# First transfers reordered, identity products ahead of the first product, and one rounding and two diagonal adds moved to VectorE

## The chip, the core and the metric

The kernel runs on one core of a Trainium2 chip. The metric is the time of one execution on the device in microseconds (us). The core's engines are TensorE (PE in the profile; its weight loads are PEld), VectorE (DVE), ScalarE (ACT), GpSimd (POOL) and SyncE (SP). Each has its own instruction stream, and they wait for each other by semaphores. Loads are issued by SP's queue, the first one and two small ones by ScalarE's.

## What is computed

Four residual layers act on `x` of 8 samples, 256 tokens and 1024 features:

```
x = x + x @ w_eff.T                                   # layer 0: w_eff is a quantized weight plus LoRA
x = x + x @ W1.T + 2 * sum_e gate_e * (x A_e) B_e     # layer 1: two of eight experts by top_k(x Wr)
x = x + x @ W2.T + b + 2 * (x As[id]) Bs[id]          # layer 2: adapter by sample
x = x + x @ weight3[id].T                             # layer 3: a weight by sample
```

In layer 0, `lora_delta = lora_B @ lora_A / 2`; `weight + lora_delta`, divided by a scale per group of 128, is replaced by the nearest of 8 code values (7 thresholds), scaled back, and `lora_delta` is added again. All is fp32.

## The kernel before

**Idea.** The weights of layers 0 to 2 are multiplied together before any `x` is touched: with the identity added to every weight ("diagonal"), the product W2' W1' W0' is one 1024 x 1024 matrix that the tokens go through once. Phase 1 builds it, phase 2 takes four groups of 512 tokens through it, then through layer 3's weight.

**Rounding.** Every fp32 operand is split into two parts of the type fp32r: ScalarE copies it into the high part (`e_hi`, `ring_hi`), VectorE subtracts that from the raw value into the low part (`minus`, L731: `e_lo`, `ring_lo`). A product is three matmuls: high by high, high by low, low by high (L992 to L994). So each piece of a weight goes landing, GpSimd's add of the identity where the piece has a diagonal block, ScalarE, VectorE, TensorE.

**Pieces and chunks.** W2 (`e_both_w`, columns U0 and up hold the adapters) is cut into column chunks 0 to 2 of 384, 512 and 128 columns, and each chunk into four pieces of two row blocks; `("w2", c, kk)` in the plan is piece kk of chunk c, and `W2_ORDER` says in which order they come. W1 comes in eight column tiles, `("w1", m)`; tile 0 in two halves, rows 512 and up first (`("w1_first",)`). In the trace, W1's tiles, W0 and the adapters `as` are all called `w_w`, W2's raw values `e_both_w`. TensorE's stream in phase 1 is a list of products, `chunk(n)`, of W1's tile m with W2's chunk c (`CHUNKS`), with `br(c)`, the product of `bcat` (`e_mid`) with W2's chunk c, after chunks 0, 2 and 4 and `lora(u)`, four short matmuls, after others. Chunk 0 is tile 0 with column chunk 0, chunk 4 tile 0 with column chunk 2, chunk 6 tile 2 with column chunk 0, chunk 9 tile 3 with column chunk 0.

**What sets the order.** `phase1_plan()` writes out by hand one list of items; ScalarE, VectorE and GpSimd each walk through it and do their part of every item. `("beat", p, r)` is round r of quantizing tiles 2p and 2p+1 of W0: rounds 0 and 1 add the LoRA delta and divide by the scale (L792, L798), round 2 starts the sum over thresholds (L800), rounds 3 to 8 add to it (L802, each behind an addition of ScalarE), the last three finish. `some(n)` takes the next n rounds. `("delta", u)` copies a LoRA product out of PSUM, `("f", n)` copies out chunk n, `("as",)` rounds the adapters of layer 2, `("thr",)` computes the thresholds. SP issues the loads in its own order, that of the plan. Chunk 4 waits for all of W2's last column chunk and for `as_lo`; every tile of W1 needs its `ring_down`.

## Time and profile before

| | us |
|---|---|
| median of 3 runs | 675.61 |
| lowest, highest | 674.91, 675.62 |
| the profiled execution's own time | 675.61 |
| its span in the profile | 673.8 |
| TensorE busy | 661.4 |
| VectorE, ScalarE, GpSimd busy | 354.1, 279.6, 89.0 |

The span runs from the first instruction to the last one; the rest of the execution's time lies around it. A row of the timeline is one instruction or a run of equal ones: start, duration, engine, line, operation, what it writes and reads, their sizes, how many, and in brackets how long the engine had been idle and what ended that. Matmuls overlap, so the distance between two starts tells the rate, and the duration is longer. An idle time that ends with "DMA" ends with the landing of that transfer.

### The profile page before, as it was taken

What the parts mean: (1) busy time and instruction counts of PE and PEld (TensorE: products, weight loads), DVE (VectorE), ACT (ScalarE), POOL (GpSimd) and SP (SyncE); (2) the same over time, 40 slices, a digit from 0 to 9 for tenths busy, and PEclk for the clock granted to TensorE, in tenths of its full rate; (3) what the DMA queues carried; (4) which work ended last, traced back from release to release, by engine and by line L of the source; (5) the groups of instructions that cost most, each with busy time, mean ns of one, the idle gap of its engine ahead of it and who ended that gap; (6) DMA issues with size and microseconds to landing.
All of it is one profiled execution on the core that took longest, in us unless ns stands there. A gap on an engine that the chain in (4) does not pass through costs nothing.

```text
span 673.8 us, 9216 instructions
## 1 busy us (share of the span) xinstructions
PE 661.4 (98%) x3264; PEld 567.8 (84%) x3264; DVE 354.1 (53%) x535; ACT 279.6 (41%) x418; POOL 89.0 (13%) x122
## 2 busy tenths in 40 slices
PE   5999999999999999999999999999999999999998
PEld 5898989999999988888889888889888888888886
DVE  5699989879971384124543222661421653411453
ACT  6556483971912371114552122562121564121353
POOL 3120225005010030001220000230000221000110
PEclk9999999999999999999999999999999999999999
DMA  9761212001000504002774000777000586000362
GB/s 317 181 196 43 82 32 63 1 0 64 1 0 1 188 12 138 1 0 94 281 231 167 0 0 31 253 245 241 0 0 0 187 284 212 27 1 1 98 233 108
DMA packets 39330, 67.59 MB, mean 100 GB/s; under 512 B 3588, under 2 KB 23044, under 8 KB 39300
## 3 DMA queue, kind: packets, MB, share of 16 engines
q1 hardware_dynamic: 34448, 59.07, 26.7%
q10 hardware_dynamic: 4852, 8.13, 3.5%
q8 instruction: 18, 0.29, 0.2%
q14 instruction: 12, 0.10, 0.1%
...
## 4 chain that ended last, share of the span: by engine, by line
PE 92%; SPq 4%; DVE 2%; ACT 1%; issue 1%; DMA 0%; POOL 0%; ACTq 0%; DVEq 0%; POOLq 0%
PE ps L992 28%; PE ps L993 28%; PE ps L994 28%; PE ps L1079 3%; PE ps L1081 1%; SPq L342 1%; SPq L367 1%; PE ps L1112 1%; ACT tmp L547 1%; SPq L366 1%; SPq L337 0%; DMA e_both_w<-w_t 0%; DVE w_w L798 0%; DVE tmp L802 0%; DVE w_w L792 0%
## 5 line engine op out<-in xcount | busy, mean ns | idle before, releaser
L992 PE MATMUL ps<-e_both,ring_hi 128*128 128x384 f32 (+3 forms) x384 | 134.6, 351 | 8.8 <-DVE e_both L731 8.0
L731 DVE TENSOR_TENSOR ring_lo<-raw,ring_hi 128x512 fp32r<-128x512 f32 x128 | 92.8, 740 | 80.8 <-ACT ring_hi L643 80.4
L994 PE MATMUL ps<-e_both,ring_lo 128*128 128x384 f32 (+3 forms) x384 | 134.1, 349 | 0.0
L643 ACT ACTIVATE ring_hi<-raw 128x512 fp32r<-128x512 f32 x128 | 79.4, 629 | 70.2 <-PE ps L994 66.6
L992 PE MATMUL ps<-x_both,e_both 128*128 128x512 f32 x256 | 101.6, 397 | 0.0
L993 PE MATMUL ps<-x_both,e_both 128*128 128x512 f32 x256 | 101.3, 396 | 0.0
L992 PE MATMUL ps<-ring_hi,e_mid 128*128 128x512 f32 x256 | 101.1, 395 | 0.0
L994 PE MATMUL ps<-ring_hi,e_mid 128*128 128x512 f32 x256 | 101.1, 395 | 0.0
L993 PE MATMUL ps<-ring_lo,e_mid 128*128 128x512 f32 x256 | 101.1, 395 | 0.0
L994 PE MATMUL ps<-x_both,e_both 128*128 128x512 f32 x256 | 101.1, 395 | 0.0
L992 PEld LDWEIGHTS ps<-e_both,ring_hi 128*128 128x128 f32 x384 | 72.8, 189 | 14.4 <-DVE e_both L731 8.0
L493 POOL TENSOR_TENSOR raw<-raw,ident 128x128 f32<-128x128 f32 x64 | 41.5, 651 | 318.7 <-DMA raw<-w_t 318.7
L994 PEld LDWEIGHTS ps<-e_both,ring_lo 128*128 128x128 f32 x384 | 72.7, 189 | 5.7
L966 DVE SCALAR_TENSOR_TENSOR e_mid<-ps,bias_col,e_mid 128x512 fp32r<-128x512 f32 x32 | 22.5, 746 | 94.7 <-ACT e_mid L689 94.7
L993 PE MATMUL ps<-e_mid,ring_hi 128*128 128x384 f32 (+2 forms) x192 | 68.6, 357 | 0.0
L993 PE MATMUL ps<-e_both,ring_hi 128*128 128x384 f32 (+2 forms) x192 | 65.5, 341 | 0.0
L802 DVE SCALAR_TENSOR_TENSOR tmp<-w_w,thr,tmp 128x1024 f32<-128x1024 f32 x48 | 60.3, 1299 | 4.4 <-ACT tmp L547 3.8
L547 ACT ACTIVATE tmp<-tmp,dif 128x1024 f32<-128x1024 f32 x48 | 54.1, 1151 | 20.3 <-DVE tmp L800 17.5
L689 ACT ACTIVATE e_mid<-ps,bias_col 128x512 fp32r<-128x512 f32 x32 | 20.4, 687 | 96.6 <-PE ps L1112 96.6
L993 PEld LDWEIGHTS ps<-ring_lo,e_mid 128*128 128x128 f32 x256 | 48.3, 189 | 11.2
L994 PEld LDWEIGHTS ps<-x_both,e_both 128*128 128x128 f32 x256 | 48.1, 188 | 11.4
L994 PEld LDWEIGHTS ps<-ring_hi,e_mid 128*128 128x128 f32 x256 | 48.3, 189 | 11.2
...
## 6 DMA issues: line engine op xcount, KB each, us to landing
...
```

The costliest lines, as they stand in the source:

```text
L342: sp.dma_start(e_lo_w[:, ks, cols], w2t[2 * kk * P:2 * (kk + 1) * P, cols].rearrange("(k p) c -> p k c", p=P)).then_inc(s_w2[4 * c + kk], 16)
L493: pool.tensor_tensor(d, d, ident[:, :], ALU.add).then_inc(w3_diag, 1)
L547: act.activation(acc[i], acc[i], ACT.Identity, bias=dif[:, LEVELS - 1 - level:LEVELS - level]).then_inc(q_add, 1)
L643: act.activation(ring_hi[:, (2 * k + h) % 4, :], raw[:, k % RAW, h * 512:(h + 1) * 512], ACT.Copy).then_inc(w3_hi, 1)
L689: act.activation(x3_hi[:, m, :], ps[:, m % 5, :], ACT.Identity, bias=bias_col[:, m:m + 1]).then_inc(x3_hi_done, 1)
L731: return dve.tensor_tensor(out, whole, hi.bitcast(F32), ALU.subtract)
L802: ins = dve.scalar_tensor_tensor(out=acc[i], in0=qf, scalar=thr[:, k:k + 1], in1=acc[i], op0=ALU.is_gt, op1=ALU.mult)
L966: dve.scalar_tensor_tensor(out=x3_lo[:, m, :], in0=ps[:, m % 5, :], scalar=bias_col[:, m:m + 1], in1=x3_hi[:, m, :].bitcast(F32), op0=ALU.add,
L992: pe.matmul(out, a[0], b_[0], start=start, stop=False, **kw)
L993: pe.matmul(out, a[0], b_[1], start=False, stop=False, **kw)
L994: return pe.matmul(out, a[1], b_[0], start=False, stop=stop, **kw)
L1079: pe.matmul(ps[:, 4 + t, 0:2 * TW].rearrange("p (h c) -> p h c", h=2), x_hi[:, k, cols], e_both[:, :, k, ecols], start=k == 0, stop=False, ...
```

## The change

1. The first transfer of ScalarE's queue was the second half of W1's tile 0 and is now W2's piece (0,2); that half is now the first transfer of SP's queue.
2. VectorE makes the high part of that half (a cast), which ScalarE did.
3. VectorE adds the identity in W1's tile 0 (`("w1_diag",)`) and in W2's row block 1 (`("w2_diag",)`), which GpSimd did. GpSimd keeps the other diagonals.
4. TensorE issues 9 products of the identity with itself, then 2, 3 and 2 more behind three waits, ahead of chunk 0.
5. W2's column chunk 2 is one transfer and one rounding of 128x8x128 instead of four, is loaded before W0's first tiles, and stands in the plan before the first rounds; `as` comes after two rounds. Five rounds stand before W1's tile 2 instead of six.
6. `lora_bt` is loaded once instead of into both halves of `xraw`, and its low part is computed from the first half.

```diff
-W2_ORDER = [(2, 3, 1, 0), (0, 1, 2, 3), (0, 1, 2, 3)]
+W2_ORDER = [(2, 3, 1, 0), (0, 1, 2, 3), (0,)]
+WARM_UP = (9, 2, 3, 2)
+DVE_DIAG = 1
...
-    plan = [("w1_first",)] + [("w2", 0, kk) for kk in W2_ORDER[0][:2]] + [("w1", 0)]
+    plan = [("w1_first",), ("w2", 0, W2_ORDER[0][0]), ("w1_diag",), ("w2", 0, W2_ORDER[0][1]), ("w1", 0), ("w2_diag",)]
...
-    plan += [("f", 2)] + deltas(0, 1, 2, 3) + [("as",)] + [("w2", 2, kk) for kk in range(4)] + some(2)
-    plan += [("br", 1)] + some(2) + [("f", 3)] + some(1) + deltas(4) + some(1) + [("w1", 2), ("f", 4)] + some(1)
-    plan += deltas(5) + some(1) + [("br", 2), ("f", 5)]
+    plan += [("f", 2)] + deltas(0, 1, 2, 3) + [("w2", 2, 0)] + some(2) + [("as",), ("br", 1)] + some(2) + [("f", 3)]
+    plan += deltas(4) + some(1) + [("w1", 2), ("f", 4)] + some(1) + deltas(5) + some(1) + [("br", 2)]
+    plan += some(1) + [("f", 5)]
...
-            for kk in W2_ORDER[0][:2]:
-                load_w2(0, kk)
+            sp.dma_start(w1_raw(0)[:, 4:KT, :], w1[512:D, 0:P].rearrange("(k p) c -> p k c", p=P)).then_inc(s_w1_first, 16)
+            load_w2(sp, 0, W2_ORDER[0][1])
...
-            act.dma_start(w1_raw(0)[:, 4:KT, :], w1[512:D, 0:P].rearrange("(k p) c -> p k c", p=P)).then_inc(s_w1_first, 16)
+            load_w2(act, 0, W2_ORDER[0][0])
...
+                    dve.wait_ge(s_w1_first, 16)
+                    dve.tensor_copy(ring(ring_hi, 0)[:, 4:KT, :], w1_raw(0)[:, 4:KT, :]).then_inc(first_up, 1)
...
+                elif what == "w1_diag":
+                    dve.wait_ge(s_w1[0], 16)
+                    dve.wait_ge(s_ident, 4)
+                    dve.tensor_tensor(w1_raw(0)[:, 0, :], w1_raw(0)[:, 0, :], ident[:, :], ALU.add
+                                      ).then_inc(first_diag, 1)
+                elif what == "w2_diag":
+                    dve.wait_ge(s_w2[DVE_DIAG // 2], 16)
+                    d = e_lo_w[:, DVE_DIAG, DVE_DIAG * P:(DVE_DIAG + 1) * P]
+                    dve.tensor_tensor(d, d, ident[:, :], ALU.add).then_inc(w2_diag_dve, 1)
...
+            def warm_up(n):
+                for _ in range(n):
+                    pe.matmul(ps[:, 7, 0:P], ident[:, :], ident[:, :], start=True, stop=True)
+
+            pe.wait_ge(s_ident, 4)
+            warm_up(WARM_UP[0])
+            pe.wait_ge(s_w1_first, 16)
+            warm_up(WARM_UP[1])
+            pe.wait_ge(s_w2[W2_ORDER[0][0]], 16)
+            warm_up(WARM_UP[2])
+            pe.wait_ge(w2_hi, 1)
+            warm_up(WARM_UP[3])
```

VectorE's stream at its start, before. `ring_lo` of 128x512 is a half of W1's tile 0, `e_both` of 2x384 a piece of W2's column chunk 0, `e_mid` is `bcat`:

```order
L731 TENSOR_TENSOR ring_lo<-w_w,ring_hi 128x512
L731 TENSOR_TENSOR e_both<-e_both_w,e_both 128x2x384 x2
L731 TENSOR_TENSOR ring_lo<-w_w,ring_hi 128x512
L731 TENSOR_TENSOR e_both<-e_both_w,e_both 128x2x384 x2
L731 TENSOR_TENSOR e_mid<-e_mid_w,e_mid 128x1024
```

The same place after (lines of the changed file):

```order
L833 CAST ring_hi<-w_w 128x512
L737 TENSOR_TENSOR ring_lo<-w_w,ring_hi 128x512
L737 TENSOR_TENSOR e_both<-e_both_w,e_both 128x2x384
L840 TENSOR_TENSOR w_w<-w_w,ident 128x128
L737 TENSOR_TENSOR e_both<-e_both_w,e_both 128x2x384
L737 TENSOR_TENSOR ring_lo<-w_w,ring_hi 128x512
L845 TENSOR_TENSOR e_both_w<-e_both_w,ident 128x128
L737 TENSOR_TENSOR e_both<-e_both_w,e_both 128x2x384 x2
L737 TENSOR_TENSOR e_mid<-e_mid_w,e_mid 128x1024
```

A cast and two adds of the identity are put in between; the order of the subtractions is the same.

VectorE's stream later on, from the end of the thresholds to the subtraction for W1's tile 3, before. `e_both<-w_w` is `as`, `e_both` of 2x128 a piece of W2's column chunk 2, `ring_lo` of 128x1024 W1's tile 2 and then tile 3:

```order
L731 TENSOR_TENSOR e_both<-w_w,e_both 128x8x128
L731 TENSOR_TENSOR e_both<-e_both_w,e_both 128x2x128 x4
L792 TENSOR_TENSOR w_w<-w_w,raw 128x1024 x2
L798 TENSOR_TENSOR w_w<-w_w,scales 128x1024 x2
L731 TENSOR_TENSOR br_lo<-ps,br_hi 128x512
L800 TENSOR_SCALAR tmp<-w_w,thr,dif 128x1024 x2
L802 SCALAR_TENSOR_TENSOR tmp<-w_w,thr,tmp 128x1024 x6
L731 TENSOR_TENSOR ring_lo<-w_w,ring_hi 128x1024
L802 SCALAR_TENSOR_TENSOR tmp<-w_w,thr,tmp 128x1024 x4
L731 TENSOR_TENSOR br_lo<-ps,br_hi 128x256
L731 TENSOR_TENSOR ring_lo<-w_w,ring_hi 128x1024
```

And after:

```order
L737 TENSOR_TENSOR e_both<-e_both_w,e_both 128x8x128
L798 TENSOR_TENSOR w_w<-w_w,raw 128x1024 x2
L804 TENSOR_TENSOR w_w<-w_w,scales 128x1024 x2
L737 TENSOR_TENSOR e_both<-w_w,e_both 128x8x128
L737 TENSOR_TENSOR br_lo<-ps,br_hi 128x512
L806 TENSOR_SCALAR tmp<-w_w,thr,dif 128x1024 x2
L808 SCALAR_TENSOR_TENSOR tmp<-w_w,thr,tmp 128x1024 x4
L737 TENSOR_TENSOR ring_lo<-w_w,ring_hi 128x1024
L808 SCALAR_TENSOR_TENSOR tmp<-w_w,thr,tmp 128x1024 x4
L737 TENSOR_TENSOR br_lo<-ps,br_hi 128x256
L808 SCALAR_TENSOR_TENSOR tmp<-w_w,thr,tmp 128x1024 x2
L737 TENSOR_TENSOR ring_lo<-w_w,ring_hi 128x1024
```

W2's last column chunk is one subtraction and stands first, `as` has moved behind rounds 0 and 1, and one round (two instructions) has moved from ahead of tile 2 to behind it, and stands after `br_lo` of 256 columns.

SP's transfers up to the first adapter, before (with the names of the arrays; `w0_w` of 128x4x128 is a half of W1's tile 0):

```order
L342 DMA e_both_w<-w2_t 128x2x384 x2
L348 DMA w0_w<-w1 128x4x128
L342 DMA e_both_w<-w2_t 128x2x384 x2
L351 DMA e_mid_w<-b_cat 128x1024
L333 DMA w0_w<-w1 128x8x128
L342 DMA e_both_w<-w2_t 128x2x512 x4
L356 DMA xraw<-lora_b_t 64x1024 x2
L358 DMA xraw<-lora_a 64x1024 x2
L359 DMA scales<-scale_log 128x64
L360 DMA cbt<-codebook 128x8
L337 DMA w0_w<-w0 128x8x128 x2
```

And after:

```order
L353 DMA w0_w<-w1 128x4x128
L337 DMA e_both_w<-w2_t 128x2x384
L355 DMA w0_w<-w1 128x4x128
L337 DMA e_both_w<-w2_t 128x2x384 x2
L358 DMA e_mid_w<-b_cat 128x1024
L346 DMA w0_w<-w1 128x8x128
L337 DMA e_both_w<-w2_t 128x2x512 x4
L362 DMA xraw<-lora_b_t 64x1024
L364 DMA xraw<-lora_a 64x1024 x2
L365 DMA scales<-scale_log 128x64
L366 DMA cbt<-codebook 128x8
L337 DMA e_both_w<-w2_t 128x8x128
```

SP now begins with W1's half instead of a piece of W2, has one `lora_bt` instead of two, and loads W2's last column chunk before W0 (before it was four transfers behind the adapters).

## Rows read from the trace of the kernel before

**Rows 1.** The head of the page.

```profile
span 673.8 us, 9216 instructions
```

**Rows 2.** TensorE's waits: engine line, releaser: us in total, times, longest.

```profile
PE ps L992 <- DVE e_both L731: 8.0, 1, 8.0
PE ps L992 <- DVE ring_lo L731: 0.8, 1, 0.8
PE ps L1005 <- ACT raw L524: 0.2, 1, 0.2
```

**Rows 3.** Timeline of PE, 8 to 14.5 us: start, duration, engine, line, operation.

```profile
8.49 0.52 PE L993 MATMUL ps<-e_both,ring_hi 128*128 128x384 f32 x1
...
11.37 0.37 PE L993 MATMUL ps<-e_both,ring_hi 128*128 128x384 f32 x1
11.57 0.34 PE L994 MATMUL ps<-e_both,ring_lo 128*128 128x384 f32 x1
...
13.69 0.34 PE L994 MATMUL ps<-e_both,ring_lo 128*128 128x384 f32 x1
14.06 0.44 PE L992 MATMUL ps<-e_both,e_mid 128*128 128x384 f32 x1
```

**Rows 4.** Timeline of DVE, 5 to 14 us.

```profile
6.99 2.09 DVE L731 TENSOR_TENSOR e_both<-e_both_w,e_both 128x768 fp32r<-128x768 f32 x2
...
10.36 1.12 DVE L731 TENSOR_TENSOR e_both<-e_both_w,e_both 128x768 fp32r<-128x768 f32 x1 [0.42 <-ACT e_both L533]
11.64 0.96 DVE L731 TENSOR_TENSOR e_both<-e_both_w,e_both 128x768 fp32r<-128x768 f32 x1 [0.15 <-ACT e_both L533]
12.60 1.41 DVE L731 TENSOR_TENSOR e_mid<-e_mid_w,e_mid 128x1024 fp32r<-128x1024 f32 x1
```

**Rows 5.** Timeline of ACT, 5 to 12 us.

```profile
5.59 0.63 ACT L567 ACTIVATE ring_hi<-w_w 128x512 fp32r<-128x512 f32 x1 [2.13 <-DMA w_w<-w]
...
9.49 0.84 ACT L533 ACTIVATE e_both<-e_both_w 128x768 fp32r<-128x768 f32 x1 [0.57 <-POOL e_both_w L451]
10.77 0.84 ACT L533 ACTIVATE e_both<-e_both_w 128x768 fp32r<-128x768 f32 x1 [0.43 <-POOL e_both_w L451]
```

**Rows 6.** Timeline of POOL, 7 to 13 us.

```profile
8.67 0.72 POOL L451 TENSOR_TENSOR e_both_w<-e_both_w,ident 128x128 f32<-128x128 f32 x1 [0.41 <-DMA e_both_w<-w_t]
9.71 0.97 POOL L451 TENSOR_TENSOR e_both_w<-e_both_w,ident 128x128 f32<-128x128 f32 x2 [0.32 <-DMA e_both_w<-w_t]
```

**Rows 7.** Timeline of DVE, 33 to 59 us.

```profile
33.07 1.23 DVE L731 TENSOR_TENSOR e_both<-w_w,e_both 128x1024 fp32r<-128x1024 f32 x1 [4.00 <-ACT e_both L593]
...
36.18 2.35 DVE L792 TENSOR_TENSOR w_w<-w_w,raw 128x1024 f32<-128x1024 f32 x2
...
41.59 1.52 DVE L800 TENSOR_SCALAR tmp<-w_w,thr,dif 128x1024 f32<-128x1024 f32 x2
43.67 7.71 DVE L802 SCALAR_TENSOR_TENSOR tmp<-w_w,thr,tmp 128x1024 f32<-128x1024 f32 x6 [0.56 <-ACT tmp L547]
51.30 1.22 DVE L731 TENSOR_TENSOR ring_lo<-w_w,ring_hi 128x1024 fp32r<-128x1024 f32 x1
...
58.10 1.23 DVE L731 TENSOR_TENSOR ring_lo<-w_w,ring_hi 128x1024 fp32r<-128x1024 f32 x1
```

**Rows 8.** Timeline of ACT at 32 us.

```profile
31.91 1.06 ACT L593 ACTIVATE e_both<-w_w 128x1024 fp32r<-128x1024 f32 x1 [0.56 <-DMA w_w<-as]
```

**Rows 9.** Timeline of PE where chunks 4, 6 and 9 start.

```profile
42.15 0.28 PE L992 MATMUL ps<-e_both,ring_hi 128*128 128x256 f32 x1
...
51.36 0.28 PE L1005 MATMUL ps<-bc_lo,bc_hi 128*128 128x256 f32 x1
51.47 0.28 PE L1007 MATMUL ps<-x_pair,bc_hi 128*128 128x256 f32 x1
52.57 0.45 PE L992 MATMUL ps<-e_both,ring_hi 128*128 128x384 f32 x1 [0.82 <-DVE ring_lo L731]
...
66.25 0.34 PE L992 MATMUL ps<-e_both,ring_hi 128*128 128x384 f32 x1
```

More of the change, by code:

```diff
@@ L222, in build @@
         s_bcat = sem("s_bcat")
-        s_w2 = [sem(f"s_w2_{i}") for i in range(12)]
+        s_w2 = [sem(f"s_w2_{i}") for i in range(9)]
         s_as = sem("s_as")
@@ L229, in build @@
         first_up = sem("first_up")
+        first_diag = sem("first_diag")
+        w2_diag_dve = sem("w2_diag_dve")
         first_down = sem("first_down")
@@ L310, in w2_piece @@
             c0, w = LEFT[c]
-            return slice(2 * kk, 2 * kk + 2), slice(c0, min(c0 + w, D))
+            return slice(2 * kk, KT if c == 2 else 2 * kk + 2), slice(c0, min(c0 + w, D))
         def w2_diagonals(c, kk):
-            return [k for k in (2 * kk, 2 * kk + 1) if CHUNK_OF[k] == c]
+            return [k for k in range(KT) if CHUNK_OF[k] == c and (c == 2 or k // 2 == kk) and k != DVE_DIAG]
         def w2_diag_count(c, kk):
@@ L326, in add_of, with load_w2 @@
             return 2 * ((LEVELS - 1) * p + level - 1) + i + 1
+        def load_w2(queue, c, kk):
+            ks, cols = w2_piece(c, kk)
+            queue.dma_start(e_lo_w[:, ks, cols],
+                         w2t[ks.start * P:ks.stop * P, cols].rearrange("(k p) c -> p k c", p=P)
+                         ).then_inc(s_w2[4 * c + kk], 16)
         @block.sync
@@ L353, in _ @@
             for kk in range(4):
-                load_w2(1, kk)
-            for half in (slice(0, R0), slice(R0, P)):
-                sp.dma_start(xraw[half, 0, :], lora_bt).then_inc(s_lora_b, 16)
+                load_w2(sp, 1, kk)
+            sp.dma_start(xraw[0:R0, 0, :], lora_bt).then_inc(s_lora_b, 16)
             for half in (slice(0, R0), slice(R0, P)):
@@ L361, in _ @@
                          ).then_inc(s_scale, 16)
+            load_w2(sp, 2, 0)
             load_w0(0)
@@ L368, in _ @@
                              las[bass.ds(a, 1)].rearrange("a p c -> p (a c)")).then_inc(s_as, 16)
-            for kk in range(4):
-                load_w2(2, kk)
             load_w1(2)
@@ L458, in _ @@
                         add_identity(e_lo_w[:, k, k * P:(k + 1) * P]).then_inc(w2_diag, 1)
-                elif item[0] == "w1":
+                elif item[0] == "w1" and item[1] > 0:
                     m = item[1]
@@ L532, in split_w2 @@
                     act.wait_ge(w2_diag, w2_diag_count(c, kk))
+                if (c, kk) == (0, DVE_DIAG // 2):
+                    act.wait_ge(w2_diag_dve, 1)
                 act.activation(e_hi[:, ks, cols], e_lo_w[:, ks, cols], ACT.Copy).then_inc(w2_hi, 1)
             def split_ring(i, whole):
-                act.wait_ge(ring_diag, i + 1)
+                if i == 0:
+                    act.wait_ge(first_diag, 1)
+                else:
+                    act.wait_ge(ring_diag, i)
                 if i >= 2:
@@ L563, in _ @@
                 what = item[0]
-                if what == "w1_first":
-                    act.wait_ge(s_w1_first, 16)
-                    act.activation(ring(ring_hi, 0)[:, 4:KT, :], w1_raw(0)[:, 4:KT, :], ACT.Copy).then_inc(first_up, 1)
-                elif what == "delta":
+                if what == "delta":
                     delta(item[1])
@@ L573, in _ @@
                 elif what == "lora":
-                    act.wait_ge(s_lora_b, 32)
-                    act.activation(stack_b[:, :], xraw[:, 0, :], ACT.Copy).then_inc(lora_hi, 1)
+                    act.wait_ge(s_lora_b, 16)
+                    act.activation(stack_b[0:R0, :], xraw[0:R0, 0, :], ACT.Copy).then_inc(lora_hi, 1)
                     act.wait_ge(s_lora_a, 32)
@@ L832, in _ @@
                     dve.wait_ge(lora_hi, 1)
-                    minus(stack_b[R0:P, :], xraw[R0:P, 0, :], stack_b[R0:P, :]).then_inc(lora_lo, 1)
+                    minus(stack_b[R0:P, :], xraw[0:R0, 0, :], stack_b[0:R0, :]).then_inc(lora_lo, 1)
                     dve.wait_ge(lora_hi, 2)
@@ L1011, in wait_left @@
             def wait_left(c, k):
-                if k % 2 == 0:
+                if c == 2 and k == 0:
+                    pe.wait_ge(w2_lo, 9)
+                    pe.wait_ge(as_lo, 1)
+                elif c < 2 and k % 2 == 0:
                     pe.wait_ge(w2_lo, 4 * c + W2_ORDER[c].index(k // 2) + 1)
-                if c == 2 and k == 0:
-                    pe.wait_ge(as_lo, 1)
             def br(c):
@@ L1040, in chunk @@
                     pe.wait_ge(a_lo, 2)
-                ks = [2 * kk + i for kk in (W2_ORDER[c] if (step, m) == (0, 0) else range(4)) for i in range(2)]
+                ks = [2 * kk + i for kk in (W2_ORDER[0] if n == 0 else range(4)) for i in range(2)]
                 for k in ks:
```

7 lines of the change are left out of this document (1 added, 6 removed).

## The prediction

> **What bounds the kernel now.** I read the head of the page first: the span is 673.8 us [rows 1], and the profiled execution took 675.61 us, which is also the median of the three runs, so 1.81 us lie around the span and every term below can be taken straight off 675.61. Then the view of waits for TensorE [rows 2]: it idles for three releasers in the whole trace, 8.0 us until its first product, 0.8 us for a `ring_lo`, 0.2 us for an evacuation. Everything else is TensorE back to back. So the change can only work in three places: how soon the first products run, how fast TensorE's clock is there, and the 0.8 us. Anything on another engine counts only if it moves one of these or makes a new wait. I call chunk 0 the first product (24 matmuls of 384 columns), B the product with `bcat` that follows it (`br(0)`), and chunk 6 the one that starts at 52.57.
>
> In TensorE's timeline of the opening [rows 3] the matmuls of chunk 0 first follow each other at (11.37 - 8.49) / 9 = 0.32 us for 384 columns, which is 1.2 GHz, and from 11.57 on at (13.69 - 11.57) / 12 = 0.177 us, the 2.4 GHz level. The engine had stood still for 8.0 us [rows 2] and worked without pause from then until the level rose at 11.37. Ten matmuls at the low level cost 10 x (0.32 - 0.177) = 1.43 us. That is what a warm start could give at most.
>
> But B starts at 14.06, and 13.69 + 0.177 = 13.87: TensorE already waits about 0.2 us there. What it waits for is the last row of the DVE timeline [rows 4]: the `bcat` rounding runs from 12.60 to 14.01. Followed back on VectorE: W2's piece (0,0) 11.64 to 12.60, W2's piece (0,1) 10.36 to 11.48, and before that VectorE idles 0.42 us for ScalarE [rows 4]. ScalarE started that piece at 9.49 after 0.57 us idle for GpSimd [rows 5], and GpSimd started its diagonal at 8.67, idle until the transfer landed [rows 6]. So the opening is bounded by a chain landing - GpSimd - ScalarE - VectorE, and TensorE's slow clock is hidden behind it but for what the wait of 0.2 us leaves.
>
> **The change part by part.** *Identity products.* 16 matmuls of 128 columns run before 8.00, where TensorE idles. Even at the 0.32 us of a 384-column matmul they take 16 x 0.32 = 5.1 us and end in time; the last two wait for the first rounding of ScalarE, and VectorE needs about 1.0 us after that (2.09 for two [rows 4]), so they delay nothing. If they raise the clock, chunk 0 runs at 0.177: its first twelve matmuls take 2.1 us. Then it waits for piece (0,1). Their worth for the end is 0 as long as B waits for `bcat`.
>
> *First transfers.* W1's second half now goes first on SP's queue, W2's piece (0,2) on ScalarE's. Both landed near each other before (ScalarE went on at 5.59 when the W1 half was there [rows 5]). The same bytes stand ahead of piece (0,1) as before (W1 256 + 256 KB, W2 three pieces of 384 KB), so I take its landing as unchanged at 8.67 [rows 6]. The first product may start up to 0.5 us sooner because ScalarE no longer rounds W1's half first (0.63 [rows 5]); this too ends in the wait for piece (0,1).
>
> *VectorE's new work.* A cast of 128x512 and two adds of 128x128. No row of before has them. The nearest are a two-source operation of 1024 columns, 1.2 us, and the one-source `TENSOR_SCALAR` of 1024 columns, 1.52 / 2 = 0.76 us [rows 7]; the cast is half as wide, so 0.4 to 0.7 us, and the adds are an eighth, 0.15 to 0.3 us each. I take 0.4 and 0.25. The cast runs before 6.26, where VectorE idled. The Trainium skill (VectorE: DVE Perf Modes, "The perf-mode tier table") says that a one-source fp32 copy between SBUF buffers runs at twice the rate of a two-source one; the two rows agree (0.76 against 1.2), and by the other reading the first product would start 0.3 us later with the same end. The adds replace GpSimd's: the one of W1 stands between pieces (0,2) and (0,3), the one of W2 just before (0,1), in the 0.42 us of idle time. It needs the landing of piece (0,0), 9.71 [rows 6]: 9.71 + 0.25 = 9.96, ahead of 10.36. Behind it on VectorE are pieces (0,1), (0,0) and `bcat`, so it would push B by whatever it passes 10.36; cover 0.4 us.
>
> *What B gains.* ScalarE gets piece (0,0) after one diagonal of GpSimd instead of two (0.97 for two [rows 6]), so it no longer idles 0.43 before 10.77 [rows 5], and VectorE's 0.15 before 11.64 [rows 4] goes. Piece (0,1) took 1.12 beside GpSimd's second add, its twin 0.96 alone [rows 4]: 0.16 more. Sum 0.31, I take 0.3. Upper end: `bcat` also falls from 1.41 to the 1.2 of its size, 0.5 in all. Lower end, below nothing: the landing is 0.3 late because small packets of W1 now go first, gain 0 to -0.2. **B: -0.3 us (-0.5 to +0.2).**
>
> *The order of the stages after B.* Before, VectorE does `as` and four pieces of W2's last chunk from 33.07 to 36.18, idle 4.00 before [rows 7], because ScalarE waited for the `as` landing until 31.91 [rows 8]. Then rounds r0 and r1 and `br_lo`, r2 at 41.59, r3 to r5 from 43.67 to 51.30, and only then W1's tile 2: `ring_lo` 51.30 to 52.53 [rows 7]. That is the 0.82 us wait of chunk 6 [rows 9]. After, the last chunk of W2 comes in one transfer before W0, is one rounding, and stands before `as`. ScalarE is free at 31.91 - 0.56 = 31.35; about 1.05 for the rounding, VectorE's 1.2 then ends at 33.6; r0, r1 and `br_lo` take 5.4 (36.18 to 41.59) and `as`, now among them, 1.2, which makes 40.2; r2 1.52, and r3 starts 0.56 after it as before, 42.3. Only r3 and r4 stand before tile 2 now, (51.30 - 43.67) / 3 = 2.5 us each: `ring_lo` 47.4 to 48.6. Chunk 6 wants it at 51.59 - 0.3 = 51.3. The wait is gone with 2.7 us to spare.
> Its price: the regular distance from 51.47 is 0.12, so chunk 6 could start at 51.59 instead of 52.57 [rows 9], 0.98 us; and its first matmul took 0.45, the same one of chunk 9 without a wait 0.34 [rows 9], 0.1 more. **Chunk 6: -1.08 us (-0.98 to -1.08).**
>
> *What is late next.* Chunk 4 starts at 42.15 [rows 9] and waits for W2's last piece and `as_lo`, now there by 40.2 at the latest and wanted at 41.85: over 1.6 us to spare. Tile 3's `ring_lo` starts at 58.10 [rows 7], wanted at 66.25 [rows 9]; one round is moved behind tile 2 and none ahead of tile 3. After that TensorE waits for nothing [rows 2], so its lead is carried to the end.
>
> **Sum:** 675.61 - 0.30 - 1.08 = 674.23; I say **674.2 us**.
>
> **The rivals.** (1) *The slow clock is worth its full price*: pieces land earlier than I think, B starts 1.4 earlier. 675.61 - 1.43 - 1.08 = 673.1. Against it: the 0.2 us wait for `bcat` that stands already. 0.10. (2) *The opening gives nothing*: the transfers at the front land later or VectorE's adds pass their cover; only chunk 6 remains, 674.5, with the lower end of B 674.7. For it: all engines take turns in 8.5 to 14. 0.23. (3) *The wait only moves* to chunk 4, if `as` comes 3 us later: 675.3. Against: 1.6 us of cover and `as` lands before its place on VectorE. 0.05. (4) *The change doesn't do what it says*: the identity products don't raise the clock. Then chunk 0 from 7.5 still has its first twelve matmuls done by 11.5, when piece (0,1) is ready, and B is hardly later: 674.4; no case of its own in time, it is inside my forecast. (5) *Slower: the clock falls.* Chunk 0 will now wait about 1.4 us for piece (0,1), near 9.9 to 11.3. The longest idle time after a rise in the trace is the 0.82 before 52.57, and the matmul after it took 0.45, the one of chunk 9 that needed no wait 0.34 [rows 9]. If the level falls in that wait and 24 of the following matmuls run at 0.32, chunk 0's other twelve and B end near 11.3 + 24 x 0.32 + 12 x 0.177 = 21.1 instead of 14.06 + 24 x 0.177 = 18.3: 675.61 + 2.8 - 1.08 = 677.3. It decides from 17 such matmuls on ((1.08 + 1.35) / 0.143). The Trainium skill (TensorE: Matmul & The Clock Gate, "HAM oscillation") warns of just this, waits for data between short bursts of matmuls that leave every burst cold; the row of the 0.82 us wait does not show it. 0.04.
>
> **How the numbers follow.** The forecast (673.9 to 674.5) has 0.55, rivals 0.10, 0.23, 0.05, 0.04, and 0.03 for something slower that I don't see. A measurement of this kernel can tell about 0.2%, 1.35 us, from no change; that bound, 674.26, runs through my forecast. Of its 0.55 I put 0.34 below. Faster: 0.34 + 0.10 + 0.01 = 0.45. Same: 0.21 + 0.22 + 0.05 + 0.01 = 0.49. Slower: 0.06. The range leaves out rival 1's end and rival 5: 673.5 to 675.2.
>
> **What would show it.** Right: VectorE's `bcat` rounding ends near 13.7 and B starts with it; chunk 0 at 0.177 from its first matmul, with a wait of about 1.4 us in its middle; `ring_lo` of tile 2 ends near 48.6 and chunk 6 follows without a gap; TensorE's waits after B are only the 0.2. Wrong: matmuls at 0.32 behind the wait in chunk 0; a landing of piece (0,1) off 8.67; a wait of chunk 4 for `as`; any new wait of TensorE after 66.

## The result and the profile after

The changed kernel takes 673.74 us (median of 14 runs, 673.62 to 674.02). The kernel before, on the same chip, takes 675.39 us (14 runs, 674.74 to 676.80). The ratio is 0.9974, with an interval of 0.9967 to 0.9982: faster by 1.65 us, 0.26%. The forecast was 674.2, between 673.5 and 675.2. The profiled executions took 675.61 and 673.76 us, with spans of 673.8 [rows 1] and 671.9 us.

The spread changed as well: the runs of before differ by 2.06 us, those of after by 0.40. The experiments show part of the reason.

Where the 1.85 us between the two profiled executions went is read from five starts on TensorE:

| start of | before | after | earlier by |
|---|---|---|---|
| chunk 0 | 8.00 | 7.75 | 0.25 |
| B | 14.06 | 13.32 | 0.74 |
| chunk 6 | 52.57 | 50.86 | 1.71 |
| chunk 9 | 66.25 | 64.43 | 1.82 |
| the last matmul | 670.09 | 668.27 | 1.82 |

So 0.74 us came in the opening, another 1.08 between B and chunk 9, and nothing after 66 us. Head and TensorE's waits of the kernel after, to be set beside [rows 1, 2]:

```profile
span 671.9 us, 9271 instructions
PE ps L1081 <- POOL br_now_lo L452: 1.6, 1, 1.6
PE ps L1010 <- DVE e_both L737: 1.2, 2, 0.9
PE ps L1023 <- ACT raw L529: 0.2, 1, 0.2
```

The 0.8 us for `ring_lo` is gone; new is a wait of 0.9 us for VectorE in the middle of chunk 0. TensorE's timeline of the opening, after (start, duration, engine, line, operation, idle time before it):

```profile
1.60 3.91 PE L1081 MATMUL ps<-ident 128*128 128x128 f32 x18 [1.60 <-POOL br_now_lo L452]
5.69 1.83 PE L1081 MATMUL ps<-ident 128*128 128x128 f32 x14 [0.17 <-DMA w_w<-w]
7.75 0.44 PE L1010 MATMUL ps<-e_both,ring_hi 128*128 128x384 f32 x1 [0.23 <-DVE e_both L737]
8.03 0.34 PE L1011 MATMUL ps<-e_both,ring_hi 128*128 128x384 f32 x1
...
9.80 0.34 PE L1012 MATMUL ps<-e_both,ring_lo 128*128 128x384 f32 x1
11.07 0.45 PE L1010 MATMUL ps<-e_both,ring_hi 128*128 128x384 f32 x1 [0.94 <-DVE e_both L737]
...
13.11 0.34 PE L1012 MATMUL ps<-e_both,ring_lo 128*128 128x384 f32 x1
13.32 0.45 PE L1010 MATMUL ps<-e_both,e_mid 128*128 128x384 f32 x1
```

```profile
5.24 0.28 PE L1081 MATMUL ps<-ident 128*128 128x128 f32 x1
```

Chunk 0 then runs at (9.80 - 8.03) / 10 = 0.177 us from the start, against 0.32 in [rows 3], and the level holds over the wait of 0.94. B starts at 13.32, 0.04 behind where matmuls at a distance of 0.177 would have it (13.11 + 0.17). VectorE in the same stretch, to be set beside [rows 4]:

```profile
5.67 0.43 DVE L833 CAST ring_hi<-w_w 128x512 fp32r<-128x512 f32 x1 [5.67 <-DMA w_w<-w]
...
7.61 0.28 DVE L840 TENSOR_TENSOR w_w<-w_w,ident 128x128 f32<-128x128 f32 x1
...
8.68 0.95 DVE L737 TENSOR_TENSOR ring_lo<-w_w,ring_hi 128x512 fp32r<-128x512 f32 x1
9.55 0.55 DVE L845 TENSOR_TENSOR e_both_w<-e_both_w,ident 128x128 f32<-128x128 f32 x1
10.06 1.99 DVE L737 TENSOR_TENSOR e_both<-e_both_w,e_both 128x768 fp32r<-128x768 f32 x2
12.04 1.22 DVE L737 TENSOR_TENSOR e_mid<-e_mid_w,e_mid 128x1024 fp32r<-128x1024 f32 x1
```

VectorE has no idle time from 5.67 to 13.26. ScalarE and GpSimd, beside [rows 5, 6]:

```profile
9.18 0.85 ACT L540 ACTIVATE e_both<-e_both_w 128x768 fp32r<-128x768 f32 x1 [0.62 <-POOL e_both_w L456]
10.21 0.84 ACT L540 ACTIVATE e_both<-e_both_w 128x768 fp32r<-128x768 f32 x1 [0.19 <-DVE e_both_w L845]
8.48 0.60 POOL L456 TENSOR_TENSOR e_both_w<-e_both_w,ident 128x128 f32<-128x128 f32 x1 [6.93 <-DMA e_both_w<-w_t]
12.15 1.43 POOL L456 TENSOR_TENSOR w_w<-w_w,ident 128x128 f32<-128x128 f32 x1 [2.20 <-DMA w_w<-w]
```

The half of W1's tile 0 that is taken up first (`w1_first`) is called W1's half from here on. Two rows of before that belong beside these are VectorE's subtraction for the other half of that tile and GpSimd's add in W1's tile 1:

```profile
9.00 0.94 DVE L731 TENSOR_TENSOR ring_lo<-w_w,ring_hi 128x512 fp32r<-128x512 f32 x1
12.34 0.58 POOL L451 TENSOR_TENSOR w_w<-w_w,ident 128x128 f32<-128x128 f32 x1 [1.66 <-DMA w_w<-w]
```

They show two things that the rest of this text needs. First, GpSimd's add for piece (0,1) starts with the landing, but its end goes by VectorE: it ends at 9.39 before and at 9.08 after, 0.39 and 0.40 us behind the start of this subtraction (9.00, 8.68), though it started 0.33 and 0.20 ahead of it. In all fourteen traces the add ends 0.31 to 0.32 us behind the end of the subtraction that VectorE had under way, after 0.50 to 0.96 us of its own. Second, `bcat`'s rounding and GpSimd's add in W1's tile 1 meet, and the one that starts first is not held up: before, GpSimd starts at 12.34 and VectorE at 12.60, the add takes 0.58 and `bcat` 1.41; after, VectorE starts at 12.04 and GpSimd at 12.15, `bcat` takes 1.22 and the add 1.43.

Later on, VectorE's and TensorE's rows that answer to [rows 7, 9]:

```profile
31.66 1.23 DVE L737 TENSOR_TENSOR e_both<-e_both_w,e_both 128x1024 fp32r<-128x1024 f32 x1 [2.48 <-ACT e_both L540]
...
37.62 1.21 DVE L737 TENSOR_TENSOR e_both<-w_w,e_both 128x1024 fp32r<-128x1024 f32 x1
...
41.44 2.48 DVE L808 SCALAR_TENSOR_TENSOR tmp<-w_w,thr,tmp 128x1024 f32<-128x1024 f32 x2 [0.56 <-ACT tmp L557]
...
46.88 1.22 DVE L737 TENSOR_TENSOR ring_lo<-w_w,ring_hi 128x1024 fp32r<-128x1024 f32 x1
50.74 0.28 PE L1025 MATMUL ps<-x_pair,bc_hi 128*128 128x256 f32 x1
50.86 0.34 PE L1010 MATMUL ps<-e_both,ring_hi 128*128 128x384 f32 x1
```

`ring_lo` of tile 2 ends at 48.1, and chunk 6 follows its predecessor at the regular 0.12, with 0.34 us for its first matmul.

### The profile page after: what moved, and what is told of

The parts are those of the page before. It is cut to its first block, busy times and chain, and to the rows that moved or that the text cites. A ratio compares the mean times of both kernels' runs of the same rounds, so it can differ in the third digit from the quotient of the medians.

```text
span 671.9 us, 9271 instructions
## 1 busy us (share of the span) xinstructions
PE 665.5 (99%) x3296; PEld 571.0 (85%) x3296; DVE 351.6 (52%) x535; ACT 278.3 (41%) x414; POOL 91.9 (14%) x120
## 3 DMA queue, kind: packets, MB, share of 16 engines
q10 hardware_dynamic: 4596, 8.26, 3.7%
## 4 chain that ended last, share of the span: by engine, by line
PE 98%; DVE 1%; DMA 1%; ACT 0%; issue 0%
PE ps L1010 30%; PE ps L1011 30%; PE ps L1012 30%; PE ps L1111 3%; PE ps L1113 1%; PE ps L1144 1%; DMA w_w<-w 1%; PE ps L1023 1%; PE ps L1025 0%; DVE e_both L737 0%; PE ps L1160 0%; PE ps L1152 0%; DVE ring_lo L737 0%; DVE tmp L999 0%; ACT e_mid_w L564 0%
## 5 line engine op out<-in xcount | busy, mean ns | idle before, releaser
L737 DVE TENSOR_TENSOR ring_lo<-raw,ring_hi 128x512 fp32r<-128x512 f32 x128 | 90.9, 725 | 82.7 <-ACT ring_hi L649 82.5
L498 POOL TENSOR_TENSOR raw<-raw,ident 128x128 f32<-128x128 f32 x64 | 43.3, 679 | 315.9 <-DMA raw<-w_t 315.9
L1012 PEld LDWEIGHTS ps<-x_both,e_both 128*128 128x128 f32 x256 | 48.1, 188 | 11.5
L1012 PEld LDWEIGHTS ps<-ring_hi,e_mid 128*128 128x128 f32 x256 | 48.2, 188 | 11.3
L1010 PEld LDWEIGHTS ps<-ring_hi,e_mid 128*128 128x128 f32 x256 | 48.2, 188 | 11.3
```

The costliest lines, as they stand in the source:

```text
L498: pool.tensor_tensor(d, d, ident[:, :], ALU.add).then_inc(w3_diag, 1)
L737: return dve.tensor_tensor(out, whole, hi.bitcast(F32), ALU.subtract)
L1010: pe.matmul(out, a[0], b_[0], start=start, stop=False, **kw)
L1012: return pe.matmul(out, a[1], b_[0], start=False, stop=stop, **kw)
```

## The experiments

The theory was that of the prediction: the opening is bounded by the chain from the landing of piece (0,1) to `bcat`, the late part takes a wait of 1.08 us away, the identity products are worth nothing while B waits for `bcat`. The rivals: the clock carries the opening's gain, the late part gives nothing for good, or the clock falls in the new wait. "Medians" below are of 8 to 14 runs; those of before in the three rounds of measurements were 675.50, 675.60 and 675.45. A difference between two kernels comes with a 95% interval from resampling their runs. The changed kernel was measured only with the result above, so each difference to it is one between two rounds, and the interval leaves out what moves between rounds, up to 0.2 us for the kernel before.

**One part alone.** The plan, the order and the single transfer of W2's column chunk 2, on the kernel before (part 5 of the change; part 6 was not run by itself):

```diff
-W2_ORDER = [(2, 3, 1, 0), (0, 1, 2, 3), (0, 1, 2, 3)]
+W2_ORDER = [(2, 3, 1, 0), (0, 1, 2, 3), (0,)]
...
-    plan += [("f", 2)] + deltas(0, 1, 2, 3) + [("as",)] + [("w2", 2, kk) for kk in range(4)] + some(2)
+    plan += [("f", 2)] + deltas(0, 1, 2, 3) + [("w2", 2, 0)] + some(2) + [("as",), ("br", 1)] + some(2) + [("f", 3)]
```

> The kernel before with only the late part of the change: W2's last column chunk in one transfer and one rounding ahead of the rounds, the adapters behind two rounds, five rounds instead of six before W1's tile 2. My theory (chunk 6's wait is worth its full 1.08 us and nothing else moves): chunk 6 starts right behind the matmul before it, B still starts near 14.06, the time is 1.08 us below before. Rival (the wait only moves to chunk 4 or to a later tile): less than 0.5 us, and a wait of TensorE in the wait view that before did not have.

Measured: 674.66 (674.20 to 674.93), ratio 0.9984 (0.9975 to 0.9993), 0.84 less than before. The `ring_lo` wait is gone, and the opening is that of before with one difference. Of its waits and TensorE's timeline:

```profile
PE ps L991 <- DVE e_both L730: 7.7, 1, 7.7
...
12.66 0.44 PE L991 MATMUL ps<-e_both,ring_hi 128*128 128x384 f32 x1
...
14.34 0.34 PE L991 MATMUL ps<-e_both,e_mid 128*128 128x384 f32 x1
```

From B to chunk 6 it takes 51.80 - 14.34 = 37.46 us, before 52.57 - 14.06 = 38.51: the late part is worth 1.05 there, as forecast. But chunk 0 ran at the low level until 12.66, 15 distances instead of the 10 of [rows 3], and B followed chunk 0 without a gap at 14.34. With nothing changed in the opening, TensorE's clock bounded it here, and not the chain to `bcat`.

**The identity products alone,** on the kernel before:

```diff
+            pe.wait_ge(s_ident, 4)
+            warm_up(9)
+            pe.wait_ge(s_w1_first, 16)
+            warm_up(2)
+            pe.wait_ge(s_w2[W2_ORDER[0][0]], 16)
+            warm_up(3)
+            pe.wait_ge(w2_hi, 1)
+            warm_up(2)
```

> The kernel before with only the identity products ahead of chunk 0. My theory (the slow clock is hidden behind the landing of piece (0,1) and VectorE's chain): chunk 0 runs at 0.177 us per matmul from its start, waits over 1 us in its middle, B starts at 13.9 to 14.06, the time is 0 to 0.2 us below before. Rival (the slow clock is paid in full): B starts near 12.7 and the time is 1.4 us below.

Measured: 675.29 (674.92 to 676.56), ratio 1.0000 (0.9991 to 1.0009). The level was up before chunk 0, and it held over a wait of 0.97 us:

```profile
11.18 0.44 PE L992 MATMUL ps<-e_both,ring_hi 128*128 128x384 f32 x1 [0.97 <-DVE e_both L731]
```

B started at 13.69, 8.47 us after W1's half had landed and ScalarE had taken it up (5.22); before it was 14.06 - 5.59 = 8.47 [rows 5]. On the chain itself the products do nothing. Chunk 6 waited 0.86 us for `ring_lo` here, as in [rows 9].

**Both of these,** the late part and the identity products, on the kernel before:

> The kernel before with the late part and the identity products, without the new transfers and without VectorE's new work. If the two add up with nothing between them: 1.1 to 1.3 us below before. If the identity products pull in a rise of the clock that in many executions comes later than in the trace of before: below that, and the times of single executions lie closer together than those of the kernel with the late part alone.

Measured: 674.31 (674.14 to 675.30), ratio 0.9982 (0.9973 to 0.9991): 0.35 less than the late part alone (interval -0.64 to +0.09). B at 13.91, again 8.47 after the start on W1's half (5.44). Zero is inside that interval; six of eleven runs of the late part alone lie above 674.6, two of eleven here.

**The whole change without the products:**

```diff
-WARM_UP = (9, 2, 3, 2)
+WARM_UP = (0, 0, 0, 0)
```

> The changed kernel without the identity products. If they are worth nothing: within 0.1 us of the changed kernel. Worked out from the changed kernel's trace, where piece (0,1) is ready at 11.05 and B starts at 13.32: chunk 0 starts at 7.75 at the low level, its first twelve matmuls end at 7.75 + 0.49 + 11 x 0.32 = 11.8, 0.7 us after piece (0,1), so the rest ends 0.7 us late: B near 13.9 to 14.1, the time 0.6 to 0.8 us above the changed kernel; later still if the level rises later.

Measured: 674.21 (673.93 to 675.43), 0.47 more than the changed kernel (+0.31 to +1.14). VectorE's `bcat` rounding runs from 12.09 to 13.32, as in the changed kernel, but B starts only when chunk 0 is through, at 13.76:

```profile
11.01 0.46 PE L1010 MATMUL ps<-e_both,ring_hi 128*128 128x384 f32 x1
...
13.59 0.34 PE L1012 MATMUL ps<-e_both,ring_lo 128*128 128x384 f32 x1
13.76 0.34 PE L1010 MATMUL ps<-e_both,e_mid 128*128 128x384 f32 x1
```

This is the sharpest comparison of the products: with the chain done at 13.3, they are worth 0.44 us in these two traces and 0.47 in the medians, though they are worth nothing on the chain. The two bounds lie 0.2 to 0.5 us apart, and the later one counts. The spread speaks for it too: 1.50 us over eleven runs without the products, 0.40 over fourteen with them.

**The old first transfers** in the changed kernel (the two lines change their queues back):

```diff
-            sp.dma_start(w1_raw(0)[:, 4:KT, :], w1[512:D, 0:P].rearrange("(k p) c -> p k c", p=P)).then_inc(s_w1_first, 16)
+            load_w2(sp, 0, W2_ORDER[0][0])
...
-            load_w2(act, 0, W2_ORDER[0][0])
+            act.dma_start(w1_raw(0)[:, 4:KT, :], w1[512:D, 0:P].rearrange("(k p) c -> p k c", p=P)).then_inc(s_w1_first, 16)
```

> The changed kernel with the first transfers as before: W1's half first on ScalarE's queue, W2's pieces (0,2) and (0,3) first on SP's. If the order of the first transfers is worth nothing (the same bytes stand ahead of piece (0,1)): B starts within 0.1 us of 13.32 and the time is within 0.1 us of the changed kernel. If the new order is what brought piece (0,1) in at 8.34 instead of 8.60: B near 13.6, the time 0.25 us above the changed kernel.

Measured: 674.06 (673.76 to 674.31), ratio 0.9976 (0.9966 to 0.9987): 0.32 more than the changed kernel (+0.21 to +0.48). B started at 13.51, 0.19 later than in the changed kernel:

```profile
5.83 0.43 DVE L833 CAST ring_hi<-w_w 128x512 fp32r<-128x512 f32 x1 [5.83 <-DMA w_w<-w]
8.74 0.50 POOL L456 TENSOR_TENSOR e_both_w<-e_both_w,ident 128x128 f32<-128x128 f32 x1 [7.19 <-DMA e_both_w<-w_t]
```

Piece (0,1) was taken up 0.26 later than in the changed kernel, at 8.74, but its add took 0.50 instead of 0.60. W1's half landed 0.16 later (5.83 against 5.67), and VectorE's stream is 0.16 later from there on: its subtraction for W1's other half starts at 8.84 instead of 8.68. So B moved with the landing of W1's half, and not with that of piece (0,1). Whether the order of the transfers makes that landing later is not shown: under the old order W1's half was taken up at 5.22 to 5.83 in six traces, under the new one at 5.51 to 5.72 in eight.

**All diagonals back on GpSimd,** the rest as changed:

```diff
-DVE_DIAG = 1
+DVE_DIAG = -1
...
-                elif item[0] == "w1" and item[1] > 0:
+                elif item[0] == "w1":
...
-                elif what == "w1_diag":
...
-                elif what == "w2_diag":
```

> The changed kernel with all diagonal adds back on GpSimd. If the adds on VectorE are what sped up the opening (ScalarE no longer waits for two adds in a row ahead of piece (0,0), and for GpSimd's 0.78 us add ahead of W1's half): ScalarE idles again about 0.4 us before piece (0,0), B starts 0.2 to 0.4 us later than 13.32. Rival (VectorE's chain is full, so 0.28 + 0.55 us less on it bring B forward): B at 13.3 or sooner, the time the same or 0.1 to 0.2 us below.

Measured: 674.34 (674.05 to 674.71), 0.61 more than the changed kernel (+0.43 to +0.72). VectorE's rows are those of before [rows 4], idle times and lengths alike, and B starts at 13.83, 8.13 us after W1's half had landed (5.70):

```profile
10.14 1.12 DVE L732 TENSOR_TENSOR e_both<-e_both_w,e_both 128x768 fp32r<-128x768 f32 x1 [0.42 <-ACT e_both L538]
...
12.37 1.41 DVE L732 TENSOR_TENSOR e_mid<-e_mid_w,e_mid 128x1024 fp32r<-128x1024 f32 x1
```

**The cast back on ScalarE,** the rest as changed:

```diff
+                if what == "w1_first":
+                    act.wait_ge(s_w1_first, 16)
+                    act.activation(ring(ring_hi, 0)[:, 4:KT, :], w1_raw(0)[:, 4:KT, :], ACT.Copy).then_inc(first_up, 1)
...
-                    dve.tensor_copy(ring(ring_hi, 0)[:, 4:KT, :], w1_raw(0)[:, 4:KT, :]).then_inc(first_up, 1)
```

> The changed kernel with W1's first half made high on ScalarE again. Theory (the cast sits in idle time of VectorE and only moves the first product, which is waited out before piece (0,1)): chunk 0 starts 0.3 to 0.5 us later than 7.75, B within 0.1 us of 13.32. Rival (ScalarE's later pieces slip too): B 0.2 us later or more.

Measured: 674.26 (674.17 to 674.41), 0.52 more than the changed kernel (+0.48 to +0.65). My expectation of B within 0.1 of 13.32 failed; it came at 13.88:

```profile
6.38 0.69 DVE L740 TENSOR_TENSOR ring_lo<-w_w,ring_hi 128x512 fp32r<-128x512 f32 x1 [6.38 <-ACT ring_hi L576]
...
9.93 0.55 DVE L845 TENSOR_TENSOR e_both_w<-e_both_w,ident 128x128 f32<-128x128 f32 x1
...
12.42 1.41 DVE L740 TENSOR_TENSOR e_mid<-e_mid_w,e_mid 128x1024 fp32r<-128x1024 f32 x1
```

VectorE starts its first subtraction at 6.38 instead of 6.13, and with the two adds on it has no idle time left to take this up: the add of W2 starts at 9.93 instead of 9.55, and piece (0,1) at 10.43 instead of 10.06. The other way to that piece was as late: beside the shifted subtractions GpSimd's add took 0.96 instead of 0.60, so ScalarE started at 9.55 instead of 9.18. Which of the two would have held alone was not separated. `bcat` takes 1.41 again instead of 1.22, and that is the rest: it starts at 12.42, and GpSimd's add in W1's tile 1 had started at 12.14. In the seven traces in which GpSimd came first there, `bcat` took 1.40 to 1.45 us and ended 1.08 to 1.09 behind the add; in the four in which VectorE came first it took 1.22 to 1.23, and the add 1.32 to 1.48. Counted from the landing of W1's half, B comes after 8.47 us before, 8.13 with the cast on VectorE alone, 8.17 with the adds alone (13.88 - 5.71), and 7.65 with both (13.32 - 5.67; 7.68 with the old transfers, 13.51 - 5.83). So each is worth 0.3 by itself, and only both together bring `bcat` ahead of GpSimd's add, for the last 0.18.

**Does the clock fall in a wait?** First with only the nine products, so that TensorE stands still between them and chunk 0:

```diff
-WARM_UP = (9, 2, 3, 2)
+WARM_UP = (9, 0, 0, 0)
```

> The changed kernel with only the nine identity products that need no transfer, so that TensorE idles from 5.5 to 7.75, about 2.2 us, twice the longest idle time after a rise that the traces show. If the clock falls in such an idle time (my slower rival): chunk 0's first matmuls are 0.32 us apart. If not: 0.177 from the first one on, and B at 13.3.

Measured, one execution: 675.12. Chunk 0 runs at the low level for 17 distances, B starts at 14.73:

```profile
1.61 4.21 PE L1081 MATMUL ps<-ident 128*128 128x128 f32 x18 [1.61 <-POOL br_now_lo L452]
7.80 0.66 PE L1010 MATMUL ps<-e_both,ring_hi 128*128 128x384 f32 x1 [1.98 <-DVE e_both L737]
```

The 18 records never left the low level, so this run can't tell a level that fell from one that had not risen. The nine alone left B later than none did (13.76), in one execution of each; since the rise comes at another place from one cold opening to the next, this does not show that the nine do harm.

Then the wait inside chunk 0 made longer, with useless additions of 128x512 on VectorE ahead of W2's add (two, then four):

```diff
                 elif what == "w2_diag":
+                    for i in range(2):
+                        same = ident[:, :].unsqueeze(1).to_broadcast([P, 4, P])
+                        dve.tensor_tensor(tmp[:, i, :].rearrange("p (c t) -> p c t", t=P), same, same, ALU.add)
```

> The changed kernel with two useless adds of 128x512 on VectorE (about 0.7 us each, written to a buffer that is not in use yet) ahead of the add for W2's row block 1, so that TensorE, whose clock has risen, waits 1.3 us longer for piece (0,1), about 2.3 instead of 0.94 us. If the idle time does not bring the clock down: 0.177 us behind it, B 1.4 us later than 13.32, the time 1.4 us above the changed kernel. If it does: matmuls 0.32 us apart behind the wait, B later still, by 0.14 us for each matmul at the low level.

Measured, one execution: 676.31. The wait became 2.08 us and the level was down behind it:

```profile
9.81 0.34 PE L1015 MATMUL ps<-e_both,ring_lo 128*128 128x384 f32 x1
12.23 0.69 PE L1013 MATMUL ps<-e_both,ring_hi 128*128 128x384 f32 x1 [2.08 <-DVE e_both L737]
12.72 0.52 PE L1014 MATMUL ps<-e_both,ring_hi 128*128 128x384 f32 x1
...
15.60 0.37 PE L1014 MATMUL ps<-e_both,ring_hi 128*128 128x384 f32 x1
15.98 0.34 PE L1013 MATMUL ps<-e_both,e_mid 128*128 128x384 f32 x1
```

Here the level had been up (0.34 at 9.81), so it did fall. The distance behind the wait is 0.49 instead of 0.29, and from 12.72 to 15.60 nine are 0.32 instead of 0.177: 0.20 + 9 x 0.143 = 1.49 us for the clock. With 12.23 - 11.07 = 1.16 for the later piece this is 2.65, and B is 2.66 later than in the changed kernel. With four additions:

> The same with four useless adds, so that TensorE waits about 3.6 us. If idle time brings the clock down it should show here or in the run with two: matmuls 0.32 us apart behind the wait. If not: 0.177 us behind it and B 2.8 us later than 13.32.

Measured, one execution: 677.43, a wait of 3.55 us from which the level was low until 16.31, B at 17.09. Rival 5's mechanism is real. The longest wait in the opening that left the level up is the 1.11 us of the run with late part and products, the shortest that brought it down 2.08. The lengths above 1.11 ran once each, and whether the length alone decides is not shown.

**The kernel before once more,** for how much of its picture is of one execution:

> The kernel before once more, for its trace: at which matmul of chunk 0 the clock rises and when B starts. If the spread of the times of the kernel before comes from when the clock rises: a rise at another matmul than the eleventh, and B at its 14.06 only if the rise comes early enough for chunk 0 to be done by then, else at chunk 0's end. If the spread comes from the landings: the rise at the eleventh again and B at the landing of piece (0,1) + 5.46.

Measured: 674.51, 1.10 less than the execution of [rows 1] with the same code:

```profile
30.97 1.05 ACT L593 ACTIVATE e_both<-w_w 128x1024 fp32r<-128x1024 f32 x1
...
50.23 1.22 DVE L731 TENSOR_TENSOR ring_lo<-w_w,ring_hi 128x1024 fp32r<-128x1024 f32 x1
51.21 0.28 PE L1007 MATMUL ps<-x_pair,bc_hi 128*128 128x256 f32 x1
51.51 0.45 PE L992 MATMUL ps<-e_both,ring_hi 128*128 128x384 f32 x1
```

The adapters had landed by 30.97, at least 0.94 sooner, so ScalarE has no idle time where [rows 8] has 0.56 and starts 0.94 earlier, `ring_lo` of tile 2 starts at 50.23 instead of 51.30 [rows 7], and of the 0.98 us ahead of chunk 6 about 0.2 is left (51.51 - 51.21 - 0.12). B started at 13.78, 8.48 us after W1's half was taken up (5.30), but 5.52 after GpSimd took up piece (0,1) (8.26), where [rows 6] has 5.39. So the wait that the late part removes varies with the landing of `as`. In the changed kernel ScalarE takes up `as` at 33.14 and VectorE only at 37.62, and `ring_lo` of tile 2 is 2.8 us early, so a landing later by a microsecond would not reach chunk 6.

**An attempt to beat the changed kernel:** piece (0,1) of W2 rounded in two parts, the one without GpSimd's add first, and `bcat` in halves.

```diff
+                if (c, kk) == (0, 1):
+                    act.activation(e_hi[:, 3:4, cols], e_lo_w[:, 3:4, cols], ACT.Copy).then_inc(w2_hi, 1)
...
+                    act.activation(bcat_up[:, 0:4, :], bcat_raw[:, 0:4, :], ACT.Copy).then_inc(bcat_hi, 1)
+                    act.activation(bcat_up[:, 4:8, :], bcat_raw[:, 4:8, :], ACT.Copy).then_inc(bcat_hi, 1)
...
+                    ks = [4, 5, 6, 7, 3, 2, 0, 1]
```

> A version that could beat the changed kernel: W2's piece (0,1) is rounded in two parts, row block 3 (which has no diagonal) without waiting for GpSimd, then row block 2, and bcat in two halves. If piece (0,1)'s chain bounds B: TensorE's wait in chunk 0 ends 0.4 us sooner, B starts 0.1 to 0.2 us sooner than 13.32 (then VectorE's own work bounds it), the time 0.1 to 0.2 us below the changed kernel. If VectorE's full chain is already the bound: B at 13.3 to 13.5, no gain or 0.1 us lost to two more instructions.

Measured: 674.13 (673.97 to 674.33), 0.39 more than the changed kernel (+0.29 to +0.50). The early half went ahead of VectorE's own W2 add, for which ScalarE now waits:

```profile
9.51 0.81 DVE L742 TENSOR_TENSOR e_both<-e_both_w,e_both 128x384 fp32r<-128x384 f32 x1
10.24 0.28 DVE L853 TENSOR_TENSOR e_both_w<-e_both_w,ident 128x128 f32<-128x128 f32 x1
...
10.64 0.85 ACT L544 ACTIVATE e_both<-e_both_w 128x768 fp32r<-128x768 f32 x1 [1.05 <-DVE e_both_w L853]
```

TensorE's wait in chunk 0 is split into 0.29 and 0.69, together 0.98 instead of 0.94. Piece (0,0), the last of chunk 0, was ready at 12.5 instead of 12.05, and chunk 0 ended late: B came at 13.69 right behind its last matmul (13.52), with the first half of `bcat` ready since 13.34. VectorE had no idle time ahead of its W2 add, so the work put in front of it delayed what ScalarE waits for.

## Why the prediction was right, and where not

**The size and the sign.** 674.2 was forecast and 673.74 measured. Stepped by medians, the late part gave 0.84, the products on top of it 0.35, cast and adds with part 6 another 0.25 (0.05 to 0.45), the new transfers 0.32: 1.76 from 675.50. The last two steps compare kernels of different rounds of measurement, and none of the three small ones is known to better than 0.15. That the sum came so near is in part luck: by these medians the late part gave less than its 1.08 and the opening three times its 0.30, and the two errors took each other up.

**Chunk 6, right.** -1.08 was forecast for the pair of traces. From B to chunk 9 it was exactly that: 66.25 - 14.06 = 52.19 before, 64.43 - 13.32 = 51.11 after. The plan on VectorE went as worked out: W2's last piece done at 32.9 (forecast 33.6), `as_lo` at 38.8 (40.2), r3 at 41.44 (42.3), `ring_lo` 46.9 to 48.1 (47.4 to 48.6). Chunk 4 started at 41.42 without a wait. What I took from one trace without asking is that the wait is the same in every execution; it was 0.86 in a second and 0.2 in a third.

**B, right in its sign, with the wrong start of the chain, and mis-sized.** Forecast -0.3, with -0.5 to +0.2 as its range; measured -0.74, outside it. I had the chain start with the landing of piece (0,1). But B keeps no fixed distance to that (5.38 to 5.52 us in four traces with the old opening in which B did not wait for chunk 0), and keeps one to the landing of W1's half (8.47, 8.47, 8.47, 8.48): GpSimd's add for the piece ends with VectorE's subtraction, however early it started. So the chain runs from W1's half through VectorE's stream. By its stages, before and after:

| from, to | before | after | gained | forecast |
|---|---|---|---|---|
| W1's half is taken up | 5.59 | 5.67 | -0.08 | not on the chain |
| to VectorE's first subtraction | 0.67 | 0.46 | 0.21 | 0 |
| to its subtraction for W1's other half | 2.74 | 2.55 | 0.19 | 0 |
| to ScalarE's start on piece (0,1) | 0.49 | 0.50 | -0.01 | 0 |
| to VectorE's piece (0,1) | 0.87 | 0.88 | -0.01 | 0 |
| piece (0,1) and the idle time behind it, piece (0,0) | 2.24 | 1.98 | 0.26 | 0.31 |
| `bcat` to B | 1.46 | 1.28 | 0.18 | 0, or 0.2 as the upper end |
| sum | | | 0.74 | 0.3 |

The term that I had worked out came as it was. The step that failed is "this too ends in the wait for piece (0,1)", by which I put an earlier start of VectorE at nothing: it was worth 0.21 and 0.19. "I take its landing as unchanged at 8.67" was off by 0.19 as well, but by the rows above it decided nothing. The wait in chunk 0 was 0.94 and not 1.4 for the same reason, piece (0,1) being ready sooner. The last 0.18 goes by who starts first, VectorE's `bcat` or GpSimd's add in W1's tile 1, and VectorE was ahead by 0.11 us.

**"Their worth for the end is 0 as long as B waits for `bcat`": the condition failed.** The sentence about the chain is true (8.47 us from W1's half to B with and without products). But chunk 0's own end stood only 0.2 us ahead of B in the trace, so a gain of 0.74 on the chain is more than the slow clock would have let through. The run without products shows that, 13.76 with `bcat` ready at 13.32. And the rise came after 9, 10 and 15 distances in three executions whose opening was the same, and in the last of these the clock was the bound. The products take that variation out. With the `as` wait gone too, this is the likely reason for the narrow spread of the changed kernel; the slow executions of the other kernels were not traced. The Trainium skill (TensorE: Matmul & The Clock Gate, "What's actually happening") says that the count of matmuls at the low level differs from run to run of one kernel. These traces agree; had I used it, the products would have had a worth of their own in the sum. For the same reason rival 4, the clock not raised, was worth more than the 0.2 us that I gave it: 674.21 measured, against 673.74.

**The cast "only moves the first product": wrong.** I wrote that before the run with the cast on ScalarE, and it is the same step as above. The cast was worth 0.5 us, since the adds take away the idle time in which a later start would have been lost, and since `bcat` then starts behind GpSimd's add. I costed each edit against the idle times of the kernel before, and not against those that the other edits leave. The sizes were fair: the cast 0.43 (forecast 0.4), the adds 0.28 and 0.55 (0.25 each). The second runs beside GpSimd's add of 9.44; it started at 9.55 and not at 9.71, behind VectorE's own work.

**GpSimd beside VectorE.** The same rows differ by who else is at work: W2's add 0.55 or 0.28, the subtraction of 768 columns 0.95 or 1.12, `bcat` 1.22 or 1.41. The Trainium skill (GPSIMD Engine Reference, "Key points") says that the two share their interfaces to SBUF and collide when VectorE reads two inputs. The three pairs fit that, each with a GpSimd add under way when the long one started. The rows say more than that they collide: the instruction that starts second is the one that takes longer, as with `bcat` in the eleven traces above. An edit that moved GpSimd's add alone was not run.

**The identity products' cost:** "at the 0.32 us of a 384-column matmul" was no bound, since a product of plain fp32 takes two records, 0.43 us at the low level. All sixteen took 5.9 us from 1.60, and were just done (7.52) when VectorE's piece was (7.75).

**Rivals.** 1, the clock's full 1.43 us, never came, because the chain takes over after 0.5. 2 and 3 did not occur. 5 did not occur at waits of 0.94 to 1.11 us, and does at 2.08; I forecast a wait of 1.4 us, and whether the level holds at that length no run shows. The Trainium skill (TensorE: Matmul & The Clock Gate, "HAM oscillation") tells of waits for data of some 3 to 5 us that leave each burst of matmuls cold. Here one of 2.08 us did it, about twice the wait that this change has.
